# The opening of a decoder kernel: attention weights in two halves, their sums on two engines, shorter waits

## The reference

```
sw   = 1 / clip(mean(|w|), 1e-5)
wq   = clip(round(w * sw), -1, 1) / sw
sx   = 127 / clip(max(|x|, last axis), 1e-5)
xq   = clip(round(x * sx), -128, 127) / sx
y    = xq @ wq.T
```

## Time and profile before

| | us |
|---|---|
| median of 3 runs | 694.37 (692.82 to 697.98) |
| the profiled execution | 696.79 |
| its span, first to last instruction | 695.0 |
| PE busy | 598.6 (86%) |
| DVE busy | 543.4 (78%) |
| ACT busy | 481.6 (69%) |
| POOL busy | 391.8 (56%) |

### The profile page before, as it was taken

One profiled execution on the slowest core, in us unless ns is written; L12 is line 12 of the kernel. 1 busy time (PEld: TensorE's weight loads), 2 busy tenths in 40 slices (PEclk: granted clock), 3 DMA queues, 4 the chain that ended last, 5 costly groups with the idle time before them and its releaser, 6 DMA issues.

```text
span 695.0 us, 20011 instructions
## 1 busy us (share of the span) xinstructions
PE 598.6 (86%) x7268; PEld 357.5 (51%) x7268; DVE 543.4 (78%) x1359; ACT 481.6 (69%) x1181; POOL 391.8 (56%) x744
## 2 busy tenths in 40 slices
PE   1689898876687879999999988789999999999984
PEld 0356665544465657644444444445565555565542
DVE  5589998889999997879999785767777777677622
ACT  3589997987687747568888775456776766776650
POOL 4323687789799969855555512335445454444422
PEclk9999999998899999999999999999999999999997
DMA  9658966311111002435444425433544433543000
GB/s 313 143 90 163 256 91 93 81 47 39 39 39 50 24 11 40 78 52 89 90 90 78 79 40 104 75 63 59 99 76 73 85 68 70 98 75 71 12 17 15
DMA packets 162818, 55.16 MB, mean 79 GB/s; under 512 B 148960, under 2 KB 160544, under 8 KB 162464
## 3 DMA queue, kind: packets, MB, share of 16 engines
q1 hardware_dynamic: 160672, 53.75, 38.5%
q0 software_dynamic: 2048, 0.14, 0.2%
HBM read 16.89 MB, written 5.24 MB: 32 GB/s over the span
## 4 chain that ended last, share of the span: by engine, by line
PE 50%; DVE 22%; DMA 8%; issue 7%; POOL 7%; ACT 3%; SPq 3%; DVEq 0%; POOLq 0%; ACTq 0%
PE bank L1315 4%; PE bank L1262 4%; DMA l1a_kT<-k_stack 3%; DVE l_neg_max L560 3%; PE bank L1248 3%; DVE mix_num_den L1524 3%; PE bank L984 3%; PE bank L1287 2%; PE bank L1269 2%; PE bank L1845 2%; PE bank L1337 2%; PE bank L1660 2%; PE bank L958 2%; PE bank L1004 2%; PE bank L1321 2%
## 5 line engine op out<-in xcount | busy, mean ns | idle before, releaser
L1163 DVE TENSOR_REDUCE l1x_neg_max<-bank 128x2 f16<-128x448 f32 (+1 forms) x192 | 116.1, 640 | 44.9 <-PE bank L1269 44.6
L1217 ACT ACTIVATE l1x_probs<-bank 128x512 f32<-128x512 f32 x192 | 104.2, 596 | 56.2 <-PE bank L1291 32.4
L871 DVE TENSOR_REDUCE l1a_neg_max<-bank 128x4 f16<-128x512 f32 x128 | 82.2, 685 | 16.1 <-PE bank L958 15.2
L918 ACT ACTIVATE l1a_probs<-bank 128x512 f32<-128x512 f32 x128 | 69.4, 595 | 21.8 <-PE bank L972 21.8
L1119 POOL DMA_DIRECT2D l1x_qT<-l1x_neg_maxT x64 | 37.3, 589 | 53.0 <-ACT l1x_neg_maxT L1213 53.0
L1660 PE MATMUL bank<-mix_xT_parts,w_ternary 128*128 128x256 f16 x384 | 52.5, 285 | 9.5 <-DVE mix_hidden L1542 9.5
L1660 PEld LDWEIGHTS bank<-mix_xT_parts,w_ternary 128*128 128x128 f16 x384 | 38.1, 102 | 21.7 <-DVE mix_hidden L1542 13.1
L560 DVE TENSOR_REDUCE l_neg_max<-bank 128x4 f16<-128x512 f32 x64 | 41.4, 671 | 8.9 <-PE bank L682 8.7
L1736 POOL TENSOR_TENSOR moe_logits<-moe_low_rank_logits,router_bias 128x6 f32<-128x6 f32 x16 | 3.3, 204 | 74.3 <-ACT moe_low_rank_logits L1813 74.3
L1474 POOL TENSOR_TENSOR mix_hidden_parts<-mix_hidden,mix_hidden_parts 128x256 f16<-128x256 f32 x48 | 37.8, 795 | 10.5 <-ACT mix_hidden_parts L1605 9.3
L629 ACT ACTIVATE l_probs<-bank 128x512 f32<-128x512 f32 x64 | 35.1, 606 | 3.4 <-PE bank L705 1.8
(11 more groups left out here) (266 smaller groups left out, 1781.3 us busy)
## 6 DMA issues: line engine op xcount, KB each, us to landing
ctx_projected<-mix_ctx_projected SPq DMA_DIRECT2D x16, 192.0 KB, 2.0
l1x_ctx_projected<-ctx_projected SPq DMA_DIRECT2D x16, 160.0 KB, 2.4
x_residual<-x_in SPq DMA_DIRECT2D x4, 512.0 KB, 8.2
mix_ctx_in<-ctx_in SPq DMA_DIRECT2D x16, 128.0 KB, 2.1
out_dram<-moe_out SPq DMA_DIRECT2D x16, 128.0 KB, 2.0
w_f<-w_in SPq DMA_DIRECT2D x2, 704.0 KB, 8.4
w_attn_f<-w_l_in SPq DMA_DIRECT2D x1, 1024.0 KB, 6.4
q_stack<-q_begin_in SPq DMA_DIRECT2D x1, 1024.0 KB, 6.1
```

Of the source, the lines that this page charges most:

```text
L871: dve.tensor_reduce(mm[:, 16 * j + 4 * s:16 * j + 4 * s + 4], b_s[c % 3][:].rearrange("p (r k) -> p r k", k=P), AX.X, ALU.max, negate=True ...
L918: act.activation(prob[:, c, :], b_st[c % 2][:], ACT.Exp).then_inc(s_exp, 1)
L1163: dve.tensor_reduce(mm[:, first:first + count], scores, AX.X, ALU.max, negate=True).then_inc(s_max, 1)
L1217: act.activation(prob[:, c, :], b_st[c % 2][:], ACT.Exp).then_inc(s_exp, 1)
```

## The change

- **Loads.** Row 0 of x alone comes first (128 KB). The weights come as two halves of 512 KB with a semaphore each: first q and v, then k and o, each half as two transfers of 256 KB whose contiguous pieces are 1 KB. Rows 1 to 3 follow, then three constants, then rows 4 to 15 in one transfer of 1536 KB. The feed-forward weights come behind it.
- **Ones.** The matrix of ones is a memset on POOL. The product with it waits for that memset and no longer for the constants.
- **Sums.** DVE sums q and k; ACT sums v and o, with the activation Abs and its accumulated output. Abs writes its elements to the place of the ternary matrix, where they are overwritten later.
- **Gains** are written ahead of the rounding, and POOL's first scales (F8s) wait for them alone.
- **First projections** wait for three ternary matrices (q, k, v); the wait for the fourth (o) stands ahead of the first output projection (T5).
- **Order.** New numbers in PHASES (l0 only), PACE and STEPS set another order within the queues.

Core of the diff:

```diff
-        F1c@-3.312 F8s@0.216 F8c.0@1.291 F8c.1@1.340 T3s@6.214"""),
+        F1c@-3.194 F8s@-0.042 F8c.0@1.285 F8c.1@1.353 T3s@5.914"""),
...
-    s_wa, s_const, s_wf = net.sem("w_attn_loaded"), net.sem("const_loaded"), net.sem("w_ffn_loaded")
-    s_zero, s_dve, s_tot, s_tern = net.sem("memory_begun"), net.sem("setup_dve_chain"), net.sem("totals_ready"), net.sem("w_attn_ternary")
+    s_wa = [net.sem(f"w_attn_loaded{m}") for m in range(2)]
+    s_const, s_wf = net.sem("const_loaded"), net.sem("w_ffn_loaded")
+    s_zero, s_dve, s_tot, s_tern = net.sem("memory_begun"), net.sem("setup_chain"), net.sem("totals_ready"), net.sem("w_attn_ternary")
...
-    consts = [(net.ones[:], dram["ones"]), (net.ident16[:], dram["ident16"]), (net.ident[:], dram["ident"]), (masks[:], dram["masks"])]
+    consts = [(net.ident16[:], dram["ident16"]), (net.ident[:], dram["ident"]), (masks[:], dram["masks"])]
...
-        net.load_x(sp, 0)
-        sp.dma_start(wa[:], dram["w_l0"]).then_inc(s_wa, 16)
+        net.load_x(sp, 0, 1)
+        for m in range(2):
+            for a in range(2):
+                sp.dma_start(wa[:, a, :].rearrange("p (m c) -> p m c", c=C)[:, m::2, :],
+                             dram["w_l0"][:, a, :].rearrange("p (m c) -> p m c", c=C)[:, m::2, :]).then_inc(s_wa[m], 16)
+        net.load_x(sp, 1, 4)
         for dst, src in consts:
             sp.dma_start(dst, src).then_inc(s_const, 16)
-        net.load_x(sp, 1)
+        net.load_x(sp, 4, NB)
...
-        for q in range(2, 4):
-            yield next(at)
-            net.load_x(sp, q)
+        yield next(at)
+        yield next(at)
...
+        pool.memset(net.ones[:], 1.0).then_inc(s_zero, 1)
...
-        dve.wait_ge(s_wa, 16)
-        for m in range(4):
+        for m in range(2):
+            if m > 0:
+                yield next(at)
+            dve.wait_ge(s_wa[m], 32)
             abs_sum(m)
+        done[0] += 2
         yield next(at)
         dve.wait_ge(s_tot, 1)
         chained(dve.tensor_scalar(mean[:, 0:4], ps[:, 0:4], 1.0 / (C * C), 1e-5, ALU.mult, ALU.max))
         dve.wait_ge(s_dve, done[0])
...
+        dve.tensor_copy(net.gain_l0[:, 1:4], mean[:, 1:4])
+        chained(dve.tensor_scalar(net.gain_l0[:, 0:1], mean[:, 0:1], 0.25, None, ALU.mult))
         for m in range(4):
             rounded(m)
-        dve.tensor_copy(net.gain_l0[:, 1:4], mean[:, 1:4])
-        chained(dve.tensor_scalar(net.gain_l0[:, 0:1], mean[:, 0:1], 0.25, None, ALU.mult))
...
-        pe.wait_ge(s_const, 16 * len(consts))
+        pe.wait_ge(s_zero, 4)
...
+        yield next(at)
+        for m in range(2, 4):
+            act.wait_ge(s_wa[m - 2], 32)
+            act.activation(mats[m][1], mats[m][0], ACT.Abs, accum_out=sums[:, m:m + 1]).then_inc(s_dve, 1)
...
-            act.wait_ge(s_dve, 8 + 2 * m)
+            act.wait_ge(s_dve, 9 + 2 * m)
...
-                    pool.wait_ge(prev.s_dve, 15)
+                    pool.wait_ge(prev.s_dve, 7)
...
-                if b % 4 == 0:
-                    dve.wait_ge(net.s_x[b // 4], 16)
+                if b in (0, 1, 4):
+                    dve.wait_ge(net.s_x[(0, 1, 4).index(b)], 16)
...
-                    pe.wait_ge(prev.s_tern, 4)
+                    pe.wait_ge(prev.s_tern, 3)
...
+                if b == 0:
+                    pe.wait_ge(prev.s_tern, 4)
...
-        def load_x(sp, q):
-
-            sp.dma_start(net.X[:, q * 4 * C:(q + 1) * 4 * C].rearrange("p (b c) -> p b c", c=C),
-                         dram["x"][4 * q:4 * q + 4].rearrange("b p c -> p b c")).then_inc(net.s_x[q], 16)
+        def load_x(sp, first, last):
+
+            sp.dma_start(net.X[:, first * C:last * C].rearrange("p (b c) -> p b c", c=C),
+                         dram["x"][first:last].rearrange("b p c -> p b c")).then_inc(net.s_x[(0, 1, 4).index(first)], 16)
 
```

More of the change, by code:

```diff
@@ L163 @@
 PACE = {
[L164 to L168 removed]
+    "l0": (-91.729, 19.87, (4.716, 6.971, 8.492, 11.987), 11.788),
+    "mix": (52.728, 7.79, (11.429, 15.313, 7.496, 17.994), 10.483),
+    "l1a": (155.651, 7.256, (10.436, 19.603, 9.301, 1.957), 11.021),
@@ new lines @@
+    ("mix", "act"): (31.719,),
+    ("mix", "dve"): (8.464,),
+    ("mix", "pe"): (37.056,),
+    ("mix", "pool"): (8.325,),
+    ("mix", "sp"): (66.465,),
+    ("l1a", "act"): (137.865,),
+    ("l1a", "dve"): (98.517,),
+    ("l1a", "pe"): (91.053,),
+    ("l1a", "pool"): (107.294,),
+    ("l1a", "sp"): (216.642,),
+    ("l1x", "act"): (327.195,),
+    ("l1x", "dve"): (313.533,),
+    ("l1x", "pe"): (217.711,),
+    ("l1x", "pool"): (333.214,),
+    ("l1x", "sp"): (260.430,),
+    ("moe", "act"): (372.266,),
@@ L202 @@
+    ("moe", "dve"): (394.603,),
+    ("moe", "pe"): (298.710,),
+    ("moe", "pool"): (376.937,),
+    ("moe", "sp"): (366.798,),
+    ("windows", "pool"): (-20.912, -55.350, -38.846, -13.098, 14.148, -35.097, -28.316, -15.869, 10.610,),
 }
@@ L245, in setup_stage @@
     cleared = [l0_vs, net.hw] + net.mm
-    ZEROED = 5 + len(cleared) + 2
+    ZEROED = 6 + len(cleared) + 2
     def sp_program(sp):
@@ L1888, in build @@
         net.sem = sem
-        net.s_x = [sem(name) for name in ("x_loaded0", "x_loaded1", "x_loaded2", "x_loaded3")]
+        net.s_x = [sem(name) for name in ("x_loaded0", "x_loaded1", "x_loaded4")]
         net.s_late, net.s_fit, net.s_ffn = sem("late_loads_done"), sem("stacks_and_windows_fitted"), sem("ffn_ternary")
@@ L1998, in shape_constants @@
         "ident": eye, "ident16": eye.astype(np.float16),
-        "masks": masks, "xwin": xwin, "ones": np.ones((P, P), np.float32),
+        "masks": masks, "xwin": xwin,
         "rope_c": rope_c.astype(np.float32), "rope_s": rope_s.astype(np.float32),
```

64 lines of the change are left out of this document (20 added, 44 removed).

## The result

The changed kernel takes 689.03 us in the median of 18 runs, the kernel before 693.62 in 18 runs beside it; the ratio is 0.9951, 95% interval 0.9930 to 0.9973, so 1.9 to 4.9 us less. Forecast were 690.2 and a range from 687.8 to 695.3. The difference of the two medians is 4.6, inside the same interval, and the expectations of the experiments count from that -4.6.

The account below looks back on a forecast made before the run. The opening's chain of waits, from weight transfer to first projections, was taken to bound the start, then l0's row pace. Terms -1.8 - 1.2 - 1.2 = -4.2 us from median 694.37 gave 690.2, range 687.8 to 695.3.

Parts of the forecast that it names:

- the terms 1.8, 1.2 and 1.2: Forecast gains in us: earlier first projections, feed-forward sums out of busy rows, large loads away from row 8.
- Step 1: Opening loads: the last attention weights land at 7.1 us instead of 7.58, at 350 GB/s with 1 KB pieces.
- rival 4: Opening: four 256 KB weight pieces go one after another, landing 5.7 us later than forecast; 695.9 us, chance 0.04.
- Step 2: Weights to first projections: row 0's F7 starts at 14.6 us instead of 16.41, a gain of 1.8.
- Step 3: Rows 2 to 3: sums of w2 and w3 leave the busy rows, gaining 1.2 us; moved scalings costed at 0.
- Step 4: Row 8: large loads move away, so its late transpose no longer stalls PE, gaining 1.2 us; no new stall.
- rival 3: Rows 2, 4, 5 and 6: moved loads make PE wait 1.2 us at each pair of transposes; 696.2 us, chance 0.12.
- (2): Transpose stalls are chance meetings and row 12's goes too, 1.9 us more gain; 688.3 us, chance 0.12.
- (1): Only the opening's head start of 1.8 us counts, sums and loads give nothing; 692.6 us, chance 0.25.
- (5): Opening: weights land no earlier, x's wait takes the rest; median within 0.7 us of 694.4, chance 0.05.
- DVE does idle for the feed-forward weights: Sign ahead of w1's sum: such idling would mean the thin cover of step 3, weights landing just in time, is gone.

Follow-up runs that it names:

- e6: Changed kernel with the first weights in one 1 MB transfer and all four sums waiting for it; 3.0 us less than the changed kernel, intervals overlap by 0.001.
- e4: Kernel before with its own opening but the changed order of everything behind it; as fast as the changed kernel.
- e7: Changed kernel, but the first projections wait for all four ternary matrices as before; median 1.0 us higher than the changed kernel by ratio, inside the intervals.
- e8: Changed kernel with x rows 8 to 15 loaded behind the feed-forward weights instead of ahead; the time shows no gain.
- e11: Changed kernel with first weights in one transfer and x rows 8 to 15 behind the feed-forward weights; same time as e6 within the intervals.
- e12: e11 with the sums of w1, w2 and w3 one to a row, instead of w1 and w2 behind each other; no better than e11.
- e2: Changed kernel with the late loads (q_stack, k_stack) back between the pairs of rows 7 and 8; 6.1 us slower, 4.12 of it an unintended GpSimd wait.
- e9: e3 with GpSimd's window-mask casts also put back, removing its unintended wait; +1.0 us against the kernel before (-1.0 to +3.1).
- e10: e2 with GpSimd's window-mask casts also put back, removing its unintended wait; 0.7 us over the changed kernel, intervals overlap.
- e1: Changed kernel with sums, means and scalings of w1, w2 and w3 back at their old places; 3.5 us slower than the changed kernel, all gain gone.
- e5: Changed kernel with its six scalings spread one to a row and row statistics back mid-row; rows 3 to 9 take 6.74 to 6.77 us instead of 6.34.
- e3: Changed kernel with sums, means, scalings and late loads all put back; row 10 to 11 takes 11.88 us, with an unintended wait of 4.11.

## Why the prediction was right, and which terms were not

The time is 1.2 from the forecast and the sign is right, but in part by luck: of the terms 1.8, 1.2 and 1.2 the first shows in no run's time clear of noise, the second comes out near 3.6 with the scalings, which were costed at 0, the third near 0.7, and these errors cancel. A fourth, the statistics' new place, was not in the sum at all. The base helped too: the forecast took 4.2 off 694.4, and over 18 runs the kernel before stands at 693.6.

**Step 1** was off by 0.3 (7.38 for 7.1), and its comparison was too mild: e6 shows that the split costs 1.2 at the landing, not the difference between 350 and 414 GB/s, 0.46. SP needs 1.96 for the four issues, and the queue moves 306 and 247 GB/s from 4 to 6 us, against 426 and 308 in e6. Whether the issues or the 1-KB pieces are to blame was not taken apart. That is rival 4's mechanism at a fifth of its price (5.7). The rule of the Trainium skill, page "DMA: Bandwidth & Descriptors", section "Bandwidth" (batch to 1 MiB), points the same way; it rests on loads issued from GpSimd, and here, issued from SP, the traces agree with its direction.

**Step 2** predicted F7 at 14.6 (its own terms add up to 14.7); it is at 14.82, and between 14.82 and 15.82 in the profiles with the same opening. That the 1.8 go through whole is not borne out: e4 has the whole gain without the opening (nor is it excluded: the intervals of both kernels are 3 us wide). e6 and e7 lean the other way (3.0 less, 1.0 more than the changed kernel), by amounts their intervals do not separate. What the traces show: 0.7 to 0.8 of the head start is lost at 19.97, since w1 and w2 need their landing (in e4, e7, e8, e11 and e12, DVE does not wait there). In e2, e9 and e10 that wait is 1.06 to 1.54 and the sum of w1 starts at 21.01 to 21.14, later than e4's 20.82: there the feed-forward weights' landing took all of the head start. What is left is smaller than what rows 0 and 1 owe to the level of TensorE, 1.3, and to the one late transpose. How much of it reaches the end stays open.

**Step 3** had the mechanism (row 2 to 3 5.59, forecast 5.9; product with ones not held) and a third of the size: e1 against the changed kernel gives 3.5, e9 against e10 3.7, instead of 1.2. I had costed the scalings at 0, since a row with one kept 6.52. But 6.34 is the pace that PE sets, 6.52 already held the wait behind the statistics, and what costs is the second scaling in one place: 1.15 in the changed kernel, 1.02 at row 9 before (0.81 of it PE's wait for the update of x), 1.11 and 1.41 of wait in e1. e5 shows these waits gone with one to a row. And I had bounded the stretch of rows 1 to 3 by PE's waits alone; in e1 a stall there came with a late transpose and with TensorE back at slow matmuls, which no row of before shows. How the 3.5 divide among these was not measured; in the profiles of e1 and the changed kernel rows 0 to 2 differ by 3.3 (2.28 of it the late transpose) and rows 8 and 9 by 2.2, while 1.1 goes the other way at rows 4 and 7.

**What the sum left out.** The prediction counted the row's phases at nothing. The statistics moved behind the row maxima. From PE's waits for these before, 0.19 to 0.21 in each of six rows, I estimate that at 1.2 in all; e5, which moved them back, lost 0.40 a row in seven. All kernels here but e5 and the one before have them moved, so their share of the time was not measured alone.

**Step 4** had mechanism and place: of the five kernels with the loads at their old place four hold row 8 for l_kT (before 1.15, e2 1.57, e3 2.05, e10 2.17; in e9 it is row 6, 1.69), of the nine with them moved none does. But of these nine seven hold row 2 or 4 instead, by 0.8 to 2.3; only the changed kernel's own profile and e12 have none. This is rival 3's mechanism, once per execution, not four times, and the four at row 4 cost at most 0.4, since PE would have waited there for the update of x. Net, e10 puts the term at 0.7 instead of 1.2, inside overlapping intervals.

**Rivals.** (2) names what happened in the profiled pair, row 12's stall gone, and it stays open: the other 13 profiles, which lack it too, all have the new phases, and the kernel before was profiled once. For an accident of that execution speaks that it took 3.2 more than the median of its 18 runs. (1) had the right doubt on the wrong term: it is the head start that no run shows in the time, and the rest that counts. (5) is out by the opening's times.

Of the signs, one against the prediction came: DVE does idle for the feed-forward weights (0.69). And outside the list row 4 to 5 is not the same but 7.49 (two scalings ahead of the update of x, which PE waits for 1.11).
